# A layer's closing normalisation moved from a stage of its own into the batch loop of the next layer

## The reference

```python
# layer 0 (attention), its end; x is (batch, 256, 512), axis 1 is the 256 rows
x = attn_out + z1ss                     # attn_out already has + bo[None, :, None]
m = jnp.mean(x, axis=1, keepdims=True)  # a mean for each column
var = jnp.var(x, axis=1, keepdims=True)
return (x - m) * jax.lax.rsqrt(var + LN_EPS)
# layer 1 (recurrent), per batch
xa = _ln(x, ln1_w, ln1_b)               # over the 512 columns of a row
...                                     # mixtures, projections r k v w g
s_new = k v + w * s                     # a scan over 256 rows, per head
...                                     # per-head norm, gate, Wo
x = x + y * g @ Wo.T
xc = _ln(x, ln2_w, ln2_b)
...                                     # a gated two-matrix block
return x + rr * (kk @ fWv.T)
```

## Time and profile before

| | us |
|---|---|
| median of 3 runs | 3781.54 (3779.95 to 3783.91) |
| the profiled execution's own time | 3791.47 |
| its span | 3789.7 |
| busy PE, share of the span | 3434.3, 91% |
| busy DVE | 2352.3, 62% |
| busy ACT | 1660.2, 44% |
| mean granted PE clock, of full speed | 0.948 |

### The profile page before, as it was taken

How to read it: one execution, slowest core, us unless ns; L and a number is a source line. 1 busy time by engine, 2 the same in 40 slices (tenths; PEclk the granted TensorE clock), 3 DMA queues, 4 the chain that set the end, 5 groups by cost and what they waited for, 6 DMA issues and landing times. The chain is left out here.

```text
span 3789.7 us, 52731 instructions
## 1 busy us (share of the span) xinstructions
PE 3434.3 (91%) x20272; PEld 2464.7 (65%) x20272; DVE 2352.3 (62%) x3754; ACT 1660.2 (44%) x3936; POOL 205.1 (5%) x303
## 2 busy tenths in 40 slices
PE   7999999999999984679988888779999999699986
PEld 6777777777777761556565555456666666477763
DVE  5665555655565555499999999547767767432212
ACT  4554444544444442344454443236666666322210
POOL 0000000000000000000000000011111100000000
PEclk9999999999999997789999998889999999899998
DMA  5332211312121202643344433130000000300013
GB/s 184 130 130 94 109 67 68 112 70 108 68 90 68 90 12 95 180 101 88 95 99 100 107 95 95 28 148 7 1 20 21 29 21 15 114 34 23 12 41 111
DMA packets 91124, 291.70 MB, mean 77 GB/s; under 512 B 19872, under 2 KB 28064, under 8 KB 66304
## 3 DMA queue, kind: packets, MB, share of 16 engines
q1 hardware_dynamic: 63152, 182.55, 16.4%
q0 software_dynamic: 10368, 75.50, 5.3%
q10 hardware_dynamic: 17360, 30.32, 2.3%
HBM read 233.82 MB, written 54.53 MB: 76 GB/s over the span
## 5 line engine op out<-in xcount | busy, mean ns | idle before, releaser
L447 ACT ACTIVATE l_prob<-l_bank,l_nmax 128x512 f32<-128x512 f32 x512 | 344.8, 685 | 215.0 <-DVE l_nmax L527 215.0
L527 DVE TENSOR_REDUCE l_nmax<-l_bank 128x1 f32<-128x512 f32 x512 | 317.9, 683 | 80.5 <-PE l_bank L375 80.4
L344 PE MATMUL l_bank<-l_x_hi,l_w_hi 128*128 128x256 f32 x1024 | 316.2, 309 | 15.8 <-DVE l_x_lo L582 15.8
L344 PE MATMUL l_bank<-l_x_lo,l_w_hi 128*128 128x256 f32 x1024 | 291.1, 284 | 0.0
L344 PE MATMUL l_bank<-l_x_hi,l_w_lo 128*128 128x256 f32 x1024 | 291.1, 284 | 0.0
L1548 DVE TENSOR_TENSOR_SCAN l_kv<-l_wx,l_kv 128x2056 f32<-128x2056 f32 x64 | 283.7, 4432 | 3.1 <-ACT l_wx L1260 3.1
L550 DVE COPY l_probT<-l_bank 128x512 f32<-128x512 f32 x256 | 173.6, 689 | 178.6 <-PE l_bank L389 178.0
L2049 ACT ACTIVATE l2a_sc<-l2a_sc,l2a_nmax 128x256 f32<-128x256 f32 x512 | 254.1, 516 | 27.5 <-DVE l2a_nmax L2119 27.5
L389 PE MATMUL l_bank<-l_ident,l_prob 128*128 128x128 f32 x2048 | 248.9, 276 | 11.4 <-DVE l_q_lo L535 6.6
L389 PEld LDWEIGHTS l_bank<-l_ident,l_prob 128*128 128x128 f32 x2048 | 225.5, 141 | 26.9 <-DVE l_k_lo L543 11.3
L411 PE MATMUL l_bank<-l_probT,l_v 128*64 128x512 f32 x1024 | 233.8, 598 | 0.0
(11 more groups left out here) (272 smaller groups left out, 7627.5 us busy)
## 6 DMA issues: line engine op xcount, KB each, us to landing
l_vb<-vd SPq DMA_DIRECT2D x64, 1024.0 KB
l_w_hi<-kept_w_hi POOLq DMA_DIRECT2D x24, 1024.0 KB, 7.8
l_w_lo<-kept_w_lo POOLq DMA_DIRECT2D x24, 1024.0 KB, 9.8
l_wv_hi<-kept_wv_hi POOLq DMA_DIRECT2D x12, 1024.0 KB, 5.1
l_wv_lo<-kept_wv_lo POOLq DMA_DIRECT2D x12, 1024.0 KB, 7.1
l_wraw<-in_l_wqk SPq DMA_DIRECT2D x8, 1024.0 KB, 9.4
kept_w_hi<-l_w_hi SPq DMA_DIRECT2D x8, 1024.0 KB, 11.6
kept_w_lo<-l_w_lo SPq DMA_DIRECT2D x8, 1024.0 KB, 13.1
```

The costliest lines, as they stand in the source:

```text
L344: mm = pe.matmul(s.ap[:, c * ROWS:(c + 1) * ROWS], a[:, kt, c, g, :], b[:, kt, c * ROWS:(c + 1) * ROWS], start=m == 0, stop=m == 3 * KT - 1)
L447: act.activation(prob[h][:, it, :], s.ap[:, :], ACT.Exp, bias=nmax[:, n % 2, it, h:h + 1], accum_out=rsum[:, n % 2, it, h:h + 1]).then_inc ...
L527: dve.tensor_reduce(nmax[:, n % 2, it, h:h + 1], s.ap[:, :], AX.X, ALU.max, negate=True).then_inc(max_ready, 1)
```

## The change

`l0_norm` is removed. Its work is done inside `l1_layer` for a batch q = b + 2, so that the loop now begins at b = -2. The centring is one product with a 256 by 256 matrix (identity minus 1/256, as two 128 by 128 blocks), `centre_rows` on PE; the bias goes through the same matrix once. ACT (`centred`) writes squares into the tile `x` and the centred rows into `an`. PE (`column_variances`) sums the squares as columns with eight one-column products, POOL takes the power -0.5 of a 128 by 4 tile, PE (`spread_deviations`) spreads it over the partitions, and DVE (`scale_rows`) writes the normalised rows into `x`, which SP stores to `x1` for the later residual. `normed(p)`, which overwrites `x`, now waits for that store. The ring of `kv` buffers goes from 3 tiles to 2. In `before.py` the names n_ belong to the removed stage.

```diff
-def l0_norm(nc, att, bo, x1):
...
-def l1_layer(nc, d, x1, u, vd, x2):
+def l1_layer(nc, d, att, x1, u, vd, x2):
-    NV, NK, RING = 2, 3, 6
+    NV, NK, RING = 2, 2, 6
-    ALL = range(-1, B + 1)
+    ALL = range(-2, B + 1)
...
+        ring += [f"nc{q}_0", f"nc{q}_1"] if q is not None else []
...
+        ring += [f"nv{q}"] if q is not None else []
...
+        ring += [f"nr{q}"] if q is not None else []
...
+                def load_att(q):
+                    if q:
+                        sp.wait_ge(x1_ready, q)
+                    sp.dma_start(an[:, :, :], att[q].rearrange("(r p) n -> p r n", p=P)).then_inc(an_in, 16)
+
+                def store_x1(q):
+                    sp.wait_ge(x1_ready, q + 1)
+                    sp.dma_start(x1[q].rearrange("(r p) n -> p r n", p=P), x[:, :, :]).then_inc(x1_stored, 16)
...
-                load_x(0)
+                load_att(0)
+                sp.dma_start(bo[:, :], d["l0_bo"]).then_inc(bo_in, 16)
...
-                load_x(1)
+                store_x1(0)
+                load_att(1)
+                store_x1(1)
+                load_att(2)
                 for n in range(NV):
                     load_v(n)
...
-                        if n == 1 and b + 2 < B:
-                            load_x(b + 2)
...
+                        if n == 6 and b + 2 < B:
+                            store_x1(b + 2)
+                        if n == 6 and b + 3 < B:
+                            load_att(b + 3)
...
+                        pool.wait_ge(nvar_ready, b + 3)
+                        pool.tensor_tensor(nrs[:, :], nrs[:, :], power[:, :], ALU.pow).then_inc(nrs_ready, 1)
...
+                def centre_rows(q):
+                    pe.wait_ge(an_in, 16 * (q + 1))
+                    for r in range(RT):
+                        s = S[f"nc{q}_{r}"]
+                        free(pe, s)
+                        for kt in range(RT):
+                            mm = pe.matmul(s.ap[:, :], block_of(r, kt)[:, :], an[:, kt, :], start=kt == 0, stop=kt == RT - 1)
+                        mm.then_inc(s.full, 1)
+
+                def column_variances(q):
+                    s = S[f"nv{q}"]
+                    free(pe, s)
+                    pe.wait_ge(nsq_ready, q + 1)
+                    for nt in range(CT):
+                        for r in range(RT):
+                            mm = pe.matmul(s.ap[:, nt:nt + 1], x[:, r, nt * P:(nt + 1) * P], ncol[:, :], start=r == 0, stop=r == RT - 1)
+                    mm.then_inc(s.full, 1)
+
+                def spread_deviations(q):
+                    s = S[f"nr{q}"]
+                    free(pe, s)
+                    pe.wait_ge(nrs_ready, q + 1)
+                    for nt in range(CT):
+                        mm = pe.matmul(s.ap[:, nt * P:(nt + 1) * P], nrs[:, nt:nt + 1].to_broadcast([P, P]), ident[:, :], start=True, stop=True)
+                    mm.then_inc(s.full, 1)
+
...
                     if 0 <= p < B:
                         mixture(p, "g")
+                    if q < B:
+                        centre_rows(q)
...
                         picks(PER * b + 2)
+                    if q < B:
+                        column_variances(q)
...
                         add_bonus(b, 1)
+                    if q < B:
+                        spread_deviations(q)
...
+                def centred(q):
+                    if 0 <= q - 1:
+                        full(act, S[f"xT{q - 1}_1"])
+                        act.wait_ge(x1_stored, 16 * q)
+                    for r in range(RT):
+                        full(act, S[f"nc{q}_{r}"])
+                    for r in range(RT):
+                        s = S[f"nc{q}_{r}"]
+                        ins = act.activation(x[:, r, :], s.ap[:, :], ACT.Square, bias=cb[:, r:r + 1])
+                        if r == RT - 1:
+                            ins.then_inc(nsq_ready, 1)
+                        act.activation(an[:, r, :], s.ap[:, :], ACT.Identity, bias=cb[:, r:r + 1]).then_inc(s.drained, 1)
                 def normed(p):
+                    act.wait_ge(x1_stored, 16 * (p + 1))
...
                         mixture(p, "g")
+                    if q < B:
+                        centred(q)
                     if now:
                         start_state(PER * b + 4)
...
+                def column_deviations(q):
+                    s = S[f"nv{q}"]
+                    full(dve, s)
+                    dve.tensor_scalar(nrs[:, :], s.ap[:, 0:CT], EPS, None, ALU.add).then_inc(s.drained, 1)
+                    drained(dve, s)
+                    dve.sem_inc(nvar_ready, 1)
+
+                def scale_rows(q):
+                    s = S[f"nr{q}"]
+                    full(dve, s)
+                    for r in range(RT):
+                        drained(dve, S[f"nc{q}_{r}"])
+                    for r in range(RT):
+                        ins = dve.tensor_tensor(x[:, r, :], an[:, r, :], s.ap[:, :], ALU.mult)
+                        if r == 0:
+                            continue
+                        ins.then_inc(s.drained, 1)
+                    drained(dve, s)
+                    dve.sem_inc(x1_ready, 1)
...
                         if n == 4 and 0 <= p < B:
                             mix(p, "w")
+                        if n == 5 and q < B:
+                            scale_rows(q)
...
+                        if n == 3 and q < B:
+                            column_deviations(q)
...
-        l0_norm(nc, att, d["l0_bo"], x1)
-        l1_layer(nc, d, x1, u, vd, x2)
+        l1_layer(nc, d, att, x1, u, vd, x2)
```

More of the change, by code:

```diff
@@ L853, in l1_layer @@
         ring += [f"r{p}_0", f"r{p}_1"] if p is not None else []
-    plan = [(label, n % RING) for n, label in enumerate(ring)]
+    plan = [("cb", RING - 1)] + [(label, n % RING) for n, label in enumerate(ring)]
     with Phase(nc, "l1") as ph:
@@ L1158, in spread_rs, with block_of, bias_rows @@
                         mm.then_inc(s.full, 1)
+                def block_of(r, kt):
+                    return own_rows if kt == r else other_rows
+                def bias_rows():
+                    s = S["cb"]
+                    pe.wait_ge(nmade, 3)
+                    pe.wait_ge(bo_in, 16)
+                    for r in range(RT):
+                        for kt in range(RT):
+                            mm = pe.matmul(s.ap[:, r:r + 1], block_of(r, kt)[:, :], bo[:, kt:kt + 1], start=kt == 0, stop=kt == RT - 1)
+                    mm.then_inc(s.full, 1)
[4 more added lines that the diff above has]
+                        free(pe, s)
+                        for kt in range(RT):
+                            mm = pe.matmul(s.ap[:, :], block_of(r, kt)[:, :], an[:, kt, :], start=kt == 0, stop=kt == RT - 1)
[14 more added lines that the diff above has]
+                        mm = pe.matmul(s.ap[:, nt * P:(nt + 1) * P], nrs[:, nt:nt + 1].to_broadcast([P, P]), ident[:, :], start=True, stop=True)
+                    mm.then_inc(s.full, 1)
                 pe.wait_ge(consts, 2)
+                bias_rows()
                 for b in ALL:
-                    p, c, now = b + 1, b - 1, 0 <= b < B
+                    q, p, c, now = b + 2, b + 1, b - 1, 0 <= b < B
                     picks(PER * b - 1)
@@ L1261, in spread_w, with bias_rows @@
                         .then_inc(wx_ready, 1)
+                def bias_rows():
+                    s = S["cb"]
+                    full(act, s)
+                    act.activation(cb[:, :], s.ap[:, 0:RT], ACT.Copy).then_inc(s.drained, 1)
+                def centred(q):
[10 more added lines that the diff above has]
+                        act.activation(an[:, r, :], s.ap[:, :], ACT.Identity, bias=cb[:, r:r + 1]).then_inc(s.drained, 1)
                 def normed(p):
+                    act.wait_ge(x1_stored, 16 * (p + 1))
                     act.wait_ge(dev_ready, p + 1)
@@ L1673, in _ @@
                             scan(unit)
-                        if n == 1 and p < B:
+                        if n == 1 and 0 <= p < B:
                             shift(p)
```

195 lines of the change are left out of this document (51 added, 144 removed).

## The result

The change made the kernel slower: 3807.99 us median of 4 runs (3805.45 to 3811.46) against 3782.72 of 4 runs before (3779.95 to 3784.0), a ratio of 1.0069, 95% interval 1.0055 to 1.0082. The forecast was 3793, 0.3% slower, in a range to 3821: the direction is right, and the loss is 25 us where 11 were forecast. Between the two profiled executions it is only 14 us (3805.45 - 3791.47). The layer itself ends 21.1 us later, and the later layers, which are the same code, took 7 us less (1305.5 against 1312.8 us). The steps are therefore judged inside the layer.

What follows compares the result with a forecast made beforehand. The prediction took DVE and PE, both nearly full in the recurrent layer, as the bound. Its terms, -92.1 + 32.5 + 61.2 + 6 + 3.3 = +10.9, put the 3781.5 median at 3793 (+0.3%), range 3764 to 3821.

Steps and rivals of the forecast that it cites:

- four steps: One middle-batch round followed through DVE and PE, 27.6 + 31.2 + 6.9 + 52.2 = 117.9 us; 3789 to 3803, chance 0.33.
- PE is dearer than its rows: Rival: longer waits bring longer low clock, one-column products emerge from under ACT; rounds of 121, 3812 to 3817, chance 0.27.
- The separate stage: From its first DMA issue to the next phase's first, 92.1 us are removed: -92.1.
- The start: Layer start: `normed(0)` waits for the `x1` store behind the weights, +23.5; added PE work +6, late v loads +3: +32.5.
- The new pieces: PE at the layer's start: centring 3.5 us, one-column products 2, spreading 0.6 after overlap; together +6.
- Batches 1 to 6: Middle batches: 642.05 us become 5 x 117.9 + 113.8 = 703.3, +61.2.
- step 4: PE from the transposition of `normed_c` to the end of `picks(8b + 6)`: 51.6 us, with spreading 52.2.
- step 3: ACT's `start_state(8b + 4)` waits for `picks(8b + 2)`, with v's copies and store behind it, until PE's transposition: 6.9 us.
- Step 2: PE from `first` to the end of `picks(8b + 2)`, without a gap: 29.15 us, centring +3.5, shorter `first` -1.5, sum 31.2.
- Batch 0: Only unit 4's spread is early against `picks(2)`: about 3.2 us, plus `scale_rows` and waiting for it, +6 (3 to 9).
- batch 7: The spread of its last unit, at 2390.85, waits for `picks` done at 2394.1: +3.3.
- The ring costs little: Rival: DVE stays ahead and waits for `picks` fall into existing waits; rounds of 112 give 3758; chance of faster 0.16.

## Why the prediction was right, and where it was short

The direction, the places of the waits and their cause were right. The size was short: 3808 lies inside the range, but above the 3789 to 3803 that the prediction gave to its own four steps (chance 0.33), and in the stretch up to 3812 that it gave to the rival "PE is dearer than its rows" (0.27). Inside the layer +21.1 us stand against +10.9. That the two are only 10 us apart is partly luck: the start came out 5.6 us cheaper than forecast, and the batches 15.8 dearer.

- **The separate stage, -92.1:** the layer's first DMA issue went from 1512.52 to 1420.46. Right.
- **The start, +32.5:** 92.1 - 65.2 = 26.9. The store was issued at 1441.8, 21.4 us after the first load (forecast 21), and `normed(0)` was +22.6 late (forecast +23.5). The new pieces and the late loads of v cost 4.3 together and not 9, and the timelines separate them. From `normed(0)` to the end of the first decays, for which the scan had waited before, it was 1584.88 - 1521.84 = 63.0 us before and 1513.8 - 1452.39 = 61.4 after: whatever the new pieces cost, put at +6, this stretch did not grow. The other 5.9 us, to the scan at 1519.73, are the first load of v, put at +3 (0 to 8). By the run with the store first the place behind Wk and Wr is 5 us of the +22.6.
- **Batches 1 to 6, +61.2:** measured +73.1, the largest miss. The place and cause were right, as the waits after and the runs with 3 buffers and with early sums show. The four steps, as means of batches 2 to 5: 27.9, 31.4, 7.8 and 53.3 us, where the prediction had 27.6, 31.2, 6.9 and 52.2. The last batch, without normalisation, took 113.9 against a forecast of 113.8. The mis-sized terms are step 4 (+1.1) and step 3 (+0.9). Step 4 was read from batch 3 of before, whose product with fWr took 7.1 us, while four of six batches there took 8.6 to 8.8; after, it took 8.4 to 8.8 in batches 1 to 5, 8.83 in the one shown. Step 3 is 6.8 in batches 1 and 6, and up to 1.6 more where the four issues of the store of v took 3.12 us and not 1.78. Step 2 is not quite without a gap: PE waits 0.86 us for ACT in it, in batch 3 before and after, and the sum contains it. In step 2 the -1.5 for a shorter `first` nearly came true (2.46 to 2.83 us in batches 2 to 5 for 3.75), but in batch 3 the slow products had only moved on, to `bonus` (3.58 for 1.99).
- **Step 3's reason** was partly wrong. It put its growth down to ACT's hold at `start_state`; moving that sum alone gave 4.5 us, under a microsecond a batch and not clear of noise. Part of its growth is the store of v, whose issues took longer in four of six batches. The late sums of 8b+5 and 8b+6, inside step 4's gapless PE, count for more.
- **Batch 0, +6, and batch 7, +3.3:** +6.9 and +6.3. In batch 7 the last unit's buffer is filled 3.2 us later after the first scan than before (73.6 against 70.4), as forecast, with 2.9 us of waiting for a sum. The other 3.1 come behind it, in waits that the prediction left out: 1.0 by the reciprocal, 1.4 more by the last product with fWv, and 0.7 up to the next phase's first statistics, which wait for a load.
- **The rivals.** "The ring costs little" is excluded: +64 us by itself. "PE is dearer than its rows", with rounds of 121 and 3812, came nearest: rounds of 120.3. Its reason holds in its clock half (2.8 us a batch in the run with the ring alone, on the same instructions); the one-column products stayed at 1.9 us.

So the removal gives 92 us, and the longer start and the loop take them back and more. The ring costs 42 us by the run with 3 buffers, and without it the same change is 17 us faster than before. What it needed beside a shorter ring were earlier sums: with them it is as fast as with a third buffer.

## What to carry to other kernels

When a ring of buffers is shortened, list for each buffer when its last reader is done, and move these readers, not the writers: here a few reordered sums on PE gave what a third buffer gave, and in the kernel before 46 of the 64 us. A stage moved into a loop costs its own time on the engine that has no gap, plus clock, however idle it was where it stood. A long wait in a profile is worth only the distance to the next thing that the waiting engine must wait for anyway, and a term read from one batch should be read in all of them before it is used.

## What the runs showed of the hardware

- Waits of PE are paid twice: with the ring alone PE's busy time for the same instructions grew from 96.9 to 99.7 us a batch, at a granted clock of 0.90 and not 0.94. The same eight products of 256 columns (`bonus`, batch 3) took 1.99 us before, at a granted clock of 1.00, and 3.58 after, at 0.54, nearly all of it at the lower of the clock's two levels, 1.2 and not 2.4 GHz. PE's longest wait ahead of them in the batch, for the reciprocal, had been 3.2 us before and 7.2 after. The windows view, before and then after:

```profile
1924.23:1926.15 1.92, 1.92 (x12) 1.43 (x9) 0.69 (x1) 1.84 (x2) 0.00 (x0) 1.00 0.52 119
```

```profile
1888.95:1892.46 3.51, 3.51 (x12) 2.52 (x8) 1.51 (x4) 2.01 (x2) 0.00 (x0) 0.54 0.32 61
```

- Sixteen one-column products take 1.95 us, 0.12 each, as much as eight transpositions (1.97).
- The four DMA issues of ACT's store of v take 1.8 us in five of seven batches before the change (2.2 and 3.3 in the others) and in two of batches 1 to 6 after it (1.9 to 3.1 in the others), and ACT's next instruction waits for them. No run says why.
